# A two-layer graph network on one core: rows of x added to the edge features by the gather's DMA, and node stages cut into more beats

## What is computed

```python
def _layer(h, edge_feats, src, dst, deg, iso, Wn, Ws, Wi, num_nodes):
    msg = (h[src] + edge_feats) @ Wn.T
    agg = jax.ops.segment_sum(msg, dst, num_segments=num_nodes)
    agg = agg / jnp.maximum(deg, 1.0)[:, None]
    self_msg = jnp.where(iso[:, None], h @ Wi.T, h @ Ws.T)
    x = agg + self_msg
    return jnp.where(x >= 0, x, RRELU_SLOPE * x)
```

## Time and profile before

| what | value |
|---|---|
| median of three executions | 1106.08 us (1105.55 to 1108.45) |
| profiled execution, its own time | 1106.56 us |
| its span in the trace | 1104.8 us |
| PE busy | 961.7 us, 87% |
| POOL busy | 760.8 us, 69% |
| DVE busy | 690.5 us, 63% |
| ACT busy | 530.1 us, 48% |
| bytes moved by DMA | 278.42 MB, 252 GB/s |

### The profile page before, as it was taken

How to read it: one execution, slowest core, us unless ns; L and a number is a source line. 1 busy time by engine, 2 the same in 40 slices (tenths; PEclk the granted TensorE clock), 3 DMA queues, 4 the chain that set the end, 5 groups by cost and what they waited for, 6 DMA issues and landing times. The chain is left out here.

```text
span 1104.8 us, 38550 instructions
## 1 busy us (share of the span) xinstructions
PE 961.7 (87%) x14625; PEld 900.1 (81%) x14625; DVE 690.5 (63%) x2323; ACT 530.1 (48%) x1211; POOL 760.8 (69%) x761
## 2 busy tenths in 40 slices
PE   1599989899999898998988997579999999999982
PEld 0488878788888888887878886479999999999982
DVE  7888877898888887886788875303233322423333
ACT  6487776777787777786777773100000000000000
POOL 8367766777747777656777657077777777777772
PEclk9999998999999998998999998689999999999996
DMA  9577886788778787787778888799988888898742
GB/s 296 162 220 277 277 284 223 252 296 272 241 265 258 234 299 235 239 290 240 224 241 274 267 279 253 231 369 280 272 264 268 277 264 266 265 273 277 208 117 53
DMA packets 154761, 278.42 MB, mean 252 GB/s; under 512 B 21538, under 2 KB 113228, under 8 KB 150604
## 3 DMA queue, kind: packets, MB, share of 16 engines
q1 hardware_dynamic: 93776, 184.33, 50.0%
q0 software_dynamic: 35776, 73.32, 23.3%
q10 hardware_dynamic: 25020, 18.25, 5.2%
HBM read 203.24 MB, written 72.57 MB: 250 GB/s over the span
## 5 line engine op out<-in xcount | busy, mean ns | idle before, releaser
L474 POOL DMA_INDIRECT rows<-x_parts_rows,idx x444 | 453.5, 1021 | 200.5 <-issue 124.0
L980 ACT CAST counts<-ps_count 128x294 f32 x992 | 438.3, 504 | 152.5 <-PE ps_count L1187 65.8
L474 POOL DMA_INDIRECT rows<-h_parts_rows,idx x288 | 277.5, 963 | 116.3 <-issue 82.0
L1199 PE MATMUL ps_dense<-counts,h_parts 128*128 128x144 bf16 x2940 | 322.8, 228 | 5.5 <-DVE sums L716 4.4
L1187 PE MATMUL ps_count<-is_code,is_lane 128*128 128x294 bf16 x992 | 301.6, 310 | 26.0 <-ACT counts L980 23.9
L1199 PE MATMUL ps_count<-counts,h_parts 128*128 128x144 bf16 x4557 | 300.6, 228 | 6.7 <-DMA counts<-counts_kept 6.7
L1199 PEld LDWEIGHTS ps_count<-counts,h_parts 128*128 128x128 bf16 x4557 | 290.5, 99 | 7.2 <-DMA counts<-counts_kept 7.0
L1138 PE MATMUL ps_win<-onehot,feats 128*128 128x40 f32 (+1 forms) x1568 | 246.0, 236 | 31.4 <-DVE sums L694 24.7
L1199 PEld LDWEIGHTS ps_dense<-counts,h_parts 128*128 128x128 bf16 x2940 | 215.7, 98 | 42.0 <-ACT counts L980 5.3
L1138 PEld LDWEIGHTS ps_win<-onehot,feats 128*128 128x128 f32 (+1 forms) x1568 | 208.9, 159 | 38.6 <-issue 30.9
L683 DVE TENSOR_SCALAR is_code<-codes,code 128x637 bf16<-128x637 f16 x496 | 197.7, 399 | 0.0
(11 more groups left out here) (97 smaller groups left out, 843.0 us busy)
## 6 DMA issues: line engine op xcount, KB each, us to landing
counts_kept<-counts SPq DMA_DIRECT2D x31, 1764.0 KB
counts<-counts_kept SPq DMA_DIRECT2D x217, 252.0 KB
feats<-in_edges_dram SPq DMA_DIRECT2D x196, 256.0 KB
rows<-x_parts_rows,idx POOLq DMA_INDIRECT x444
h_parts_rows<-row_parts ACTq DMA_DIRECT2D x17, 288.0 KB
...
rows<-h_parts_rows,idx POOLq DMA_INDIRECT x288
```

The costliest lines, as they stand in the source:

```text
L474: nc.gpsimd.indirect_dma_start(rows[:, SUB * slot + c, :], None, table[:, :], bass.IndirectOffsetOnAxis(ap=indices[:, c:c + 1], axis=0)).t ...
L980: nc.scalar.copy(counts[:, j % BUFFERS, :, at(offset + first, count)], ps_count[:, q % BANKS, 0:count * TILES].rearrange("p (r t) -> p t r ...
L1199: last = nc.tensor.matmul(bank, h_parts[:, t, k, :], counts[:, b, t, :], start=(t == 0 and k == 0), stop=(t == TILES - 1 and k == PARTS - 1))
```

## The change

In layer 0 the edge features of a window are loaded first, and the gather then adds x's f32 rows (512 bytes each) to them in SBUF with an accumulating indirect DMA (`compute_op=ALU.add`). PE has then one operand less: the products of `rows` are gone from layer 0, and so is the table `x_parts_rows`. The edge features have a ring of 12 windows; in layer 1 the same memory holds `rows`, a ring of 8. A window to be split waits on DVE for its gather. The stages of a node trio are laid out by a table of beats (`STAGE`): in layer 0 DVE's `cut_h` goes one beat later, its last part two, and the last two trios have a shorter layout; the products with Ws and Wi (`self_products`) are apart from those with the sums (`sum_products`) and in layer 1 come before `READY`; ACT copies the former, and DVE scales and adds in one instruction for each tile. The last trio has 2 tiles and not 3, and the last window 2 chunks and not 4. The windows that are split are chosen anew (78 again; 44 of them gather).

```diff
-    FEATS = 5
-    ROWS = 5
+    FEATS = 12
+    ROWS = 8
...
+    REAL_CHUNKS = -(-EDGES // P)
...
-    SPLIT = [k for k in range(WINDOWS) if k % 5 in (1, 3)]
...
-    BEATS = [max(READY[0][-1] + 7, len(BUILDS)), READY[1][-1] + 5]
-    x_parts_rows = nc.dram_tensor("x_parts_rows", (COLS, PARTS * D), bf16, kind="Internal").ap()
+    SLOW = {"inputs": 0, "degrees": 1, "invert": 2, "products": 3, "activate": 4, "parts": 5, "last_part": 6,
+            "turn": 5, "keep": 6, "keep_turned": 7}
+    FAST = {"inputs": 0, "degrees": 1, "invert": 1, "products": 2, "activate": 2, "parts": 3, "last_part": 3,
+            "turn": 3, "keep": 3, "keep_turned": 4}
+    STAGE = {(0, name, READY[0][u] + (FAST if u >= TRIOS - 2 else SLOW)[name]): u
+             for u in range(TRIOS) for name in SLOW}
+    LATER = {"inputs": -2, "self": -1, "products": 1, "activate": 2, "normalize": 3}
+    STAGE.update({(1, name, max(READY[1][u] + after, 0)): u for u in range(TRIOS) for name, after in LATER.items()})
+    assert len(STAGE) == TRIOS * (len(SLOW) + len(LATER))
+    BEATS = [max(READY[0][-1] + 6, len(BUILDS)), READY[1][-1] + 5]
...
+    SPLIT, share = [], 0.0
+    for k in range(WINDOWS):
+        share += SPLIT_RATE
+        if share >= 1 and all((0, name, k - 2) not in STAGE for name in ("inputs", "activate", "parts")):
+            SPLIT.append(k)
+            share -= 1
+    SPLIT_OF = {k: i for i, k in enumerate(SPLIT)}
...
-        rows = sb("rows", [P, ROWS * SUB, PARTS * D], bf16)
...
+        rows = feats[:, :, :].rearrange("p c d -> p (c d)").bitcast(bf16).rearrange("p (c d) -> p c d", d=PARTS * D)
...
+            first_loads = GATHERED[:2] + [k for k in range(FEATS) if k not in GATHERED[:2]]
+            for k in first_loads[:2]:
+                load_feats(chunk_of(k), k)
...
+            for k in first_loads[2:]:
+                load_feats(chunk_of(k), k)
...
-            sp.wait_ge(setup_step, setup_marks["zeros"])
-            for r in (0, P + TILES * P):
-                sp.dma_start(x_parts_rows[r:r + P, :],
-                             zeros[:, 0:PARTS * D // 2].bitcast(bf16)).then_inc(x_parts_stored, 16)
-            for i in range(CUTS):
-                r = slice(P + P * CUT * i, P + P * CUT * (i + 1))
-                sp.wait_ge(x_part[0], i + 1)
-                sp.wait_ge(x_part[1], i + 1)
-                sp.wait_ge(x_part[2], i + 1)
-                sp.dma_start(by_tile(x_parts_rows[r, :]),
-                             h_parts[:, CUT * i:CUT * (i + 1), :, :].rearrange("p t k d -> p t (k d)")
-                             ).then_inc(x_parts_stored, 16)
-            for k in range(FEATS):
-                load_feats(chunk_of(k), k)
...
+            def add_rows(indices, slot, done, count=SUB):
+
+                for c in range(count):
+                    nc.gpsimd.indirect_dma_start(
+                        feats[:, SUB * slot + c, :], None, x_rows[:, :],
+                        bass.IndirectOffsetOnAxis(ap=indices[:, c:c + 1], axis=0),
+                        compute_op=ALU.add).then_inc(rows_gathered[done], 16)
+
+            def add_window_rows(r):
+
+                n = GATHERED[r]
+                pool.wait_ge(feats_loaded[n % FEATS], 16 * (n // FEATS + 1))
+                chunk = chunk_of(n)
+                add_rows(idx[:, chunk:chunk + SUB], n % FEATS, r % ROWS, chunks_in(n))
 
...
-            for r, n in enumerate(GATHERED[:RAW]):
-                for c in range(SUB):
-                    nc.gpsimd.indirect_dma_start(
-                        raw_rows(SUB * r + c), None, x_rows[:, :],
-                        bass.IndirectOffsetOnAxis(ap=idx[:, chunk_of(n) + c:chunk_of(n) + c + 1], axis=0)
-                    ).then_inc(rows_gathered[r], 16)
+            for r in range(RAW):
+                add_window_rows(r)
...
-                    layer = int(n >= WINDOWS)
-                    if r == RAW or (layer and GATHERED[r - 1] < WINDOWS):
-                        stored(layer)
-                    if r >= ROWS:
-                        pool.wait_ge(window_summed, GATHERED[r - ROWS] + 1)
+                    pool.wait_ge(window_summed, GATHERED[r - ROWS] + 1)
+                    if n < WINDOWS:
+                        add_window_rows(r)
+                        continue
+                    if GATHERED[r - 1] < WINDOWS:
+                        pool.wait_ge(window_summed, WINDOWS)
+                        pool.wait_ge(parts_stored, 16 * TRIOS)
                     chunk = chunk_of(n)
-                    gather((x_parts_rows, h_parts_rows)[layer], idx[:, chunk:chunk + SUB], r % ROWS)
+                    gather(idx[:, chunk:chunk + SUB], r % ROWS, chunks_in(n))
...
+                if k in GATHER_OF:
+                    dve.wait_ge(rows_gathered[GATHER_OF[k] % ROWS], rows_of(GATHER_OF[k]))
...
-                dve.wait_ge(mean_made, 3 * (n + 1))
-                nc.vector.tensor_tensor(total[:, :], ps_self[:, 0, 0:TRIO], mean[:, :],
-                                        ALU.add).then_inc(total_made, 1)
-                if layer == 0 and not zero(u):
+                c = slice(0, real(u) * D)
+                dve.wait_ge(node_out, n + 1)
+                dve.wait_ge(self_kept, n + 1)
...
+                for t in range(real(u)):
+                    d = slice(t * D, (t + 1) * D)
+                    nc.vector.scalar_tensor_tensor(total[:, d], ps_node[:, 0, d], deg_inv[:, u, t:t + 1],
+                                                   self_sums[:, d], ALU.mult, ALU.add).then_inc(total_made, 1)
...
+            def node_stage0(beat):
+
+                if (0, "last_part", beat) in STAGE and (0, "parts", beat) not in STAGE:
+                    last_part(STAGE[0, "last_part", beat])
+                if (0, "invert", beat) in STAGE:
+                    invert(STAGE[0, "invert", beat])
+                if (0, "activate", beat) in STAGE:
+                    activate(0, STAGE[0, "activate", beat])
+                if (0, "parts", beat) in STAGE:
+                    cut_h(STAGE[0, "parts", beat])
+                    if (0, "last_part", beat) in STAGE:
+                        last_part(STAGE[0, "last_part", beat])
+                if (0, "inputs", beat) in STAGE:
+                    node_inputs(0, STAGE[0, "inputs", beat])
...
+                        dve.sem_inc(sums_ready, 1)
...
+                nc.scalar.copy(self_sums[:, c], ps_self[:, 0, c]).then_inc(self_kept, 1)
...
-                if raw:
-                    lefts += [(raw_rows(r), hot)]
-                elif gathered:
-                    lefts += [(rows[:, r, i * D:(i + 1) * D], upper(hot)) for i in range(PARTS)]
+                else:
+                    lefts = [(rows[:, r, i * D:(i + 1) * D], upper(hot)) for i in range(PARTS)]
...
-            def node_products(layer, u):
+            def self_products(layer, u):
 
                 n = layer * TRIOS + u
-                if zero(u):
+                if u == 0:
                     pe.wait_ge(wts_loaded, 16 * 3 * (layer + 1))
-                if not zero(n):
+                if n:
+                    pe.wait_ge(self_kept, n)
+                if layer == 0:
+
+                    pe.wait_ge(deg_clamped, u + 1)
+                pe.wait_ge(node_in, n + 1)
+                for t in range(real(u)):
+                    for k, left in ((1, h_con), (2, h_in)):
+                        last = nc.tensor.matmul(ps_self[:, 0, t * D:(t + 1) * D], left[:, t * P:(t + 1) * P],
+                                                wts[:, k, :], start=k == 1, stop=k == 2)
+                last.then_inc(self_out, 1)
+
+            def sum_products(layer, u):
+
+                n = layer * TRIOS + u
+                if n:
                     pe.wait_ge(h_made, n)
                     pe.wait_ge(turned_kept, u if layer == 0 else TRIOS)
-                if layer == 0:
-
-                    pe.wait_ge(deg_clamped, u + 1)
-                pe.wait_ge(node_in, n + 1)
-                for t in range(3):
-                    lefts = (sums[:, SUM, at(u * TRIO + t * P, P)], h_con[:, t * P:(t + 1) * P],
-                             h_in[:, t * P:(t + 1) * P])
-                    for k, left in enumerate(lefts):
-                        last = nc.tensor.matmul((ps_self if k else ps_node)[:, 0, t * D:(t + 1) * D],
-                                                left, wts[:, k, :],
-                                                start=(k != 2), stop=(k != 1))
+                if layer:
+                    pe.wait_ge(sums_ready, u + 1)
+                for t in range(real(u)):
+                    last = nc.tensor.matmul(ps_node[:, 0, t * D:(t + 1) * D], sums[:, SUM, at(u * TRIO + t * P, P)],
+                                            wts[:, 0, :], start=True, stop=True)
                 last.then_inc(node_out, 1)
 
...
```

301 lines of the change are left out of this document (154 added, 147 removed).

## The result

The changed kernel takes 1304.73 us, the median of four executions (1302.16 to 1306.21), against 1105.82 us before: a ratio of 1.1796, with a 95% interval of 1.1762 to 1.183. The profiled execution took 1306.21 us, with a span of 1304.3 us. The forecast was 1043 us and faster. Behind a ratio, its 95% interval stands in brackets; a ratio is taken to the kernel before, run beside the one in question.

What follows compares the result with a forecast made beforehand. Layer 0 was taken as bound by two close limits, POOL's 1.301 us a gather and the pace of PE, DVE and ACT. Layer 0's end at 645, then passage, layer 1, end and 1.76 us summed to 1043 us; range 1018 to 1115 us.

Steps and rivals of the forecast that it cites:

- POOL in layer 0: Layer 0: 462 gathers at 1.301 us each, accumulating at +0 (bounds +0 and +0.48 us), so POOL ends at 620 us.
- The dear rival: POOL, layer 0: each of 442 gathers costs y more, slower from y = 0.20 us; chance 0.21, shared with DMA bound.
- Start, +1.5 us: Start of layer 0: two loads of edge features ahead of x's rows cost +1.5 us, bounds 0 and +3.
- The pace of the three engines: PE, DVE and ACT in layer 0: 36.6 us a step without waiting for POOL, 16 steps, ending at 641 us.
- two limits that disturb each other: Layer 0: 4 us added because POOL's end at 620 and the three engines' at 641 us disturb each other.
- the sentence on 88%: DVE in layer 0: keeps its 530.6 us busy in some 600 us, 88%, so PE's saving isn't credited whole.
- Split windows' wait, nothing: DVE's wait for gathers of split windows in layer 0 costs nothing, covered by POOL running up to eight gathered windows ahead.
- Passage, -3 us: Passage from layer 0 to layer 1: 3 us shorter, bounds 0 and -6.
- Layer 1, -2.5 us: Layer 1: two gathers of 1.267 us less, -2.5 us.
- End, -6 us: Behind the last gather: less DVE preparation, 4 of PE's 18 passes remain, smaller tile-wise work; -6.1 us of 20.0.
- The DMA rival: DMA engines bound layer 0: at 0.7 us a gather, kernel at 1117 us; chance 0.21, shared with a dear gather.
- A rival without a chance: POOL in layer 0 held by the loads it now waits for, so its rest would stay; no chance of its own.

Runs made afterwards that it cites:

- e5: The changed kernel with its accumulating gather of layer 0 taking 64 rows in place of 128; 1250.16 us, one execution.
- e6: The changed kernel with a plain gather over the edge features and 64 rows in place of 128; 1060.7 us, one execution.
- e1_plain: The changed kernel with compute_op taken off layer 0's gather, so x's rows overwrite the edge features; 1063.3 us, ratio 0.9627 to the kernel before.
- e3_plain_split_ungathered: e1_plain with the windows split on DVE chosen only among those that don't gather (64 in place of 78); 1062.55 us, ratio 0.9606.
- e9_earlier_self: e4 with the inputs and self products of layer 1 one beat earlier; 1084.89 us, ratio 0.9837 to the kernel before.
- e4: The changed kernel with the old gather, table, rings of 5 and products of rows back, new node stages kept; 1091.75 us, ratio 0.9876.

## Why the prediction was wrong

**The step that failed** is in *POOL in layer 0*: the accumulate's price on POOL, of which the prediction says "I take +0, the nearest row, since the same 128 rows are addressed". The price is +0.60 us, above even its upper bound, "half as much again, +0.48 us". The nearest row was the nearest in destination and size, but not in kind. The rows named, 0.94 us for 512 and for 768 bytes, do show that a plain gather's price doesn't hang on the bytes, and for the accumulating one the runs show the same (1546 ns with 256 bytes a row). That it does not hang on the kind of transfer either, no row said. The upper bound was a guess of the same sort: one more part beside two like ones, for which no row stood. And the stated range did not even hold it: it ends at 1115 us, where +0.48 us gives 1230.

**The dear rival was the right one** as to where the time is lost, and its chance of some 0.2 was too small for an operation that no row shows, on the engine of which the text itself says that +0.1 us is 44 us. With its own formula, layer 0 ends at 620 + 442 x 0.60 = 885 us, and the terms behind it give 1283 us in place of the 1306.21 us of the profiled run. Layer 0 ended at 905.0, 20 us later. 9 of these are the first 20 gathers, which the formula priced as plain and which end at 47.3 us, where it had 38.5. 8 more are the other 442, which took 1.92 us each and not 1.901, and the rest lies behind the last gather, where the sum had 6 us and 9.6 were needed. (By its own rows, the "some 7 us" there were 5.9 before, 1 us on the sum.) The condition for slower, y over 0.20 us, was right to name, and the kernel was three times beyond it.

**The page of the Trainium skill** that spoke against this part held as far as it went. "DMA: Bandwidth & Descriptors", section "Rules for kernel authors", has the accumulate read its destination and write it later, and the section "SWDGE vs HWDGE vs iDMA" has software on GpSimd compute the descriptors. This case's queue agrees in so far as an accumulating gather leaves in more packets, 112 more at 128 rows (below). But the mechanism that I drew from it, one more descriptor for each row, would make the surcharge proportional to the rows, and e5 and e6 show that it is not: 520 ns remain of 598 at half the rows. What POOL does in the part that doesn't hang on the rows stays open.

**With the plain price, the rest of the sum can be read from e1_plain,** which is the kernel that the forecast in truth describes. Layer 0 ends at 659.7 us where 645 was forecast, inside its 620 to 665. The profiled execution, the fastest of four, takes 1058.82 us against 1043, 16 us more, and the median, 1063.3, is 20 us more. Of the 16, layer 0 has 14.7, and the end 3.7, while the passage gives back 2.7.

- *Start, +1.5 us:* the first window is at 45.30 us in place of 44.69, +0.6.
- *The pace of the three engines:* 36.6 us a step was forecast. In e1_plain the four light steps take 38.1, 36.0, 36.1 (422.80 to 458.87) and 38.1 us and the twelve others 38.1 on the mean, so the mean step is 37.8 us ((650.29 - 45.30) / 16). That is 1.2 x 16 = 19 us, where +4 stood for two limits that disturb each other, and this is nearly all that layer 0 is late. Which of the two limits holds the steps isn't shown. POOL's idle time of 167.0 us was 28 us more than its pauses, and DVE was busy 529 of 619 us, as the sentence on 88% had warned; but in e3_plain_split_ungathered DVE had 18 us less to do, and nothing was gained.
- *Split windows' wait, nothing:* right with plain gathers (no idle time before the split in e1_plain). In the changed kernel the cover is gone, as the text said it would be.
- *Passage, -3 us:* -6.0 in the changed kernel (16.8 in place of 22.8 us), at the bound, and about as much in e1_plain. *Layer 1, -2.5 us:* -2.4 in e1_plain, and -0.1 in the changed kernel, whose gathers there took 972 ns and not 963 (9 ns x 286 = 2.6 us).
- *End, -6 us:* -2.4. That of PE's passes "4 remain" was wrong: the 8 passes of the self products are early in the plan, but still behind the last window on PE. e9_earlier_self, one beat earlier, has 13.7 us where the sum had 13.9.

**The DMA rival** fell. The share in layer 0 is 0.69 in the changed kernel and 0.73 in e1_plain, both under the 0.77 of before. My cost of 0.46 us of the 16 engines for a gather was too low, though. The queue's row on the page of the changed kernel, and on that of e1_plain (packets, MB, share of 16 engines):

```profile
q0 software_dynamic: 80256, 58.44, 26.8%
```

```profile
q0 software_dynamic: 28512, 58.44, 19.4%
```

That is 0.268 x 1304.3 = 349.6 us against 0.194 x 1057.0 = 205.1 us, and 144.5 us over 462 gathers are 0.31 us more for each. With 0.342 us for each of the 286 in layer 1, a plain one of 512-byte rows takes (205.1 - 97.8) / 462 = 0.23 us, an accumulating one 0.54. With POOL at 1.92 us for each gather it didn't come to bear.

**A rival without a chance:** that POOL is held by the loads it waits for I gave "no chance of its own", because SP loads 12 windows ahead. For the ring of 12 that was right, with 31.9 us of it left; at five slots the same mechanism makes the kernel 11.8% slower than the one before, even with plain gathers. The sentence was true for a reason, the depth, that deserved a price.

Of the 199 us lost, then: the node stages and the shorter last trio and window gave 14 (e4), the plain form of the new gather with its deep ring another 28 (1091.75 to 1063.3), and the accumulate took 241.
